# Writing the bf16 copies of the expert weights during the prefix subtiles, and moving a LayerNorm, in a gated-linear-attention and mixture-of-experts layer

## What is computed

```python
# layer 0, x: [4, 4096, 2048] f32
x = x + attn(layernorm(x), Wq, Wk, Wv, Wo, norm_w)
x = x + ffn(layernorm(x), gate_w, w1, w2, w3, ws1, ws2, ws3)

def attn(x, ...):                    # 16 heads of 128 channels, chunks of 64 tokens
    q = silu(x @ Wq.T); f = sigmoid(x @ Wk.T); log_f = log_sigmoid(f); v = x @ Wv.T
    o = chunked_gla(q, v, log_f)     # S_t = diag(exp(log_f_t)) S_{t-1} + outer(1 - exp(log_f_t), v_t)
    return rmsnorm(o, norm_w) @ Wo.T #   o_t = q_t @ S_t, one state S per head

def ffn(x, ...):                     # 8 experts, top 2, and one shared expert, each 2048 -> 1024 -> 2048
    weights, idx = top_k(softmax(x @ gate_w.T), 2)
    y = sum over experts e of comb[:, e] * ((silu(x @ w1[e].T) * (x @ w3[e].T)) @ w2[e].T)
    return y + silu(x @ ws1.T) * (x @ ws3.T) @ ws2.T
```

## Time and profile before

| | us |
|---|---|
| two runs | 8881.81 and 9365.76, median 9123.78 |
| profiled execution | 8866.93 |
| its span, slowest core (core 1) | 8865.2 |
| spans of the eight cores | 8808.3 to 8865.2 |
| busy in the span: TensorE | 5739.3 (65%) |
| VectorE | 2370.4 (27%) |
| ScalarE | 1152.4 (13%) |

### The profile page before, as it was taken

One profiled execution on the slowest core, in us unless ns is written; L12 is line 12 of the kernel. 1 busy time (PEld: TensorE's weight loads), 2 busy tenths in 40 slices (PEclk: granted clock), 3 DMA queues, 4 the chain that ended last, 5 costly groups with the idle time before them and its releaser, 6 DMA issues.

```text
span 8865.2 us, 86241 instructions; the slowest of 8 cores (8808.3 to 8865.2 us)
## 1 busy us (share of the span) xinstructions
PE 5739.3 (65%) x26192; PEld 2628.4 (30%) x26192; DVE 2370.4 (27%) x7284; ACT 1152.4 (13%) x2288; POOL 275.7 (3%) x522
## 2 busy tenths in 40 slices
PE   5454545465565655666677776665877766577877
PEld 3131313232222222232233332322333342233333
DVE  3434343444300100124321112343111124421111
ACT  1111111111100000111111111111111111101111
POOL 0000000000000000000000000000000000000000
PEclk8676767676787878876688998766999986688998
DMA  5131313132577577552243333322333332143332
GB/s 83 32 57 29 60 27 62 30 66 43 104 161 168 136 161 170 132 112 36 41 119 114 114 114 105 67 45 61 124 114 114 114 91 41 31 119 114 114 119 95
DMA packets 203967, 806.76 MB, mean 91 GB/s; under 512 B 22272, under 2 KB 22288, under 8 KB 189200
## 3 DMA queue, kind: packets, MB, share of 16 engines
q0 software_dynamic: 77008, 331.42, 21.9%
q1 hardware_dynamic: 126528, 469.82, 14.6%
HBM read 1002.51 MB, written 130.02 MB: 128 GB/s over the span
## 4 chain that ended last, share of the span: by engine, by line
PE 53%; DVE 16%; DMA 15%; issue 7%; ACT 6%; SPq 2%; DVEq 1%; POOL 1%; ACTq 0%; POOLq 0%
PE ps L76 51%; DMA wB<-w_t 3%; DVE Em L76 3%; DMA wB<-w3c 3%; DMA wC<-w_t 3%; DVE Ssb L76 2%; DVE Ep L76 2%; DVE krem L76 2%; PE psb L76 2%; DMA w2c<-wC 2%; SPq L76 2%; ACT Em L76 2%; ACT krem L76 1%; ACT fm L76 1%; DMA wB<-wk_t 1%
## 5 line engine op out<-in xcount | busy, mean ns | idle before, releaser
L76 PE MATMUL ps<-fm,wA 128*128 128x512 bf16 x5632 | 1497.8, 427 | 917.5 <-DMA wB<-w_t 487.3
L76 PE MATMUL ps<-fm,wB 128*128 128x512 bf16 x6656 | 1758.8, 425 | 37.3 <-DMA wB<-wk_t 26.4
L76 PEld LDWEIGHTS ps<-fm,wA 128*128 128x128 bf16 x5632 | 594.8, 107 | 1764.4 <-issue 1254.8
L76 PEld LDWEIGHTS ps<-fm,wB 128*128 128x128 bf16 x6656 | 702.8, 107 | 1009.1 <-issue 398.4
L76 DVE TENSOR_TENSOR vcb<-sqb,ps 128x512 bf16<-128x512 bf16 x288 | 198.2, 688 | 2671.7 <-PE ps L76 2671.7
L76 PE MATMUL ps<-ob,vcb 128*128 128x512 bf16 x2304 | 623.5, 405 | 262.2 <-ACT Em L76 133.3
L76 DVE SCALAR_TENSOR_TENSOR Ssb<-Ssb,dec,ps 128x128 f32<-128x128 f32 x1024 | 355.7, 347 | 1341.5 <-PE ps L76 1277.6
L76 PE MATMUL ps<-wC,fm 128*128 128x256 bf16 x4096 | 510.9, 291 | 117.3 <-DVE vcb L76 94.4
L76 PE MATMUL ps<-vcb,krtm 64*128 64x128 bf16 x1024 | 247.5, 242 | 502.9 <-ACT krtm L76 246.6
L76 ACT ACTIVATE sqb<-ps 128x512 bf16<-128x512 f32 x352 | 209.6, 595 | 2597.5 <-PE ps L76 2597.5
L76 PE MATMUL ps<-wC,vcb 128*128 128x512 bf16 x2304 | 520.8, 379 | 0.0
(11 more groups left out here) (91 smaller groups left out, 3273.8 us busy)
## 6 DMA issues: line engine op xcount, KB each, us to landing
wA<-w1c SPq DMA_DIRECT2D x216, 512.0 KB, 3.7
wB<-w3c SPq DMA_DIRECT2D x216, 512.0 KB, 4.6
wC<-wv_t POOLq DMA_DIRECT2D x64, 1024.0 KB, 9.4
wB<-wk_t POOLq DMA_DIRECT2D x128, 512.0 KB, 5.3
ob<-w2c SPq DMA_DIRECT2D x108, 512.0 KB, 5.2
wC<-w2c SPq DMA_DIRECT2D x108, 512.0 KB, 8.9
wA<-w_t POOLq DMA_DIRECT2D x72, 512.0 KB, 7.8
wB<-w_t POOLq DMA_DIRECT2D x72, 512.0 KB, 10.7
```

The costliest lines, as they stand in the source:

```text
L76: ins = getattr(eng, name)(*a, **k)
```

## The change

- `_precache_steps` is new. It puts jobs on the queues, 216 in all (matrix, expert, block): POOL loads a block as bf16 into one of four slots of `y1g`, once the store that used the slot four jobs ago and the load just before have landed; SP writes it to the bf16 copy. Seven jobs are queued at the start of every prefix `_pair_chunks`, seven more after the last pair of a prefix subtile.
- All FFN passes load the copies on SP. The loads wait for the write-backs of their blocks. The write-backs of the first pass are gone, and three waits for them.
- `_ffn` computes the LayerNorm of the next own subtile after the gate phase of the last expert, ahead of the w2 phases of experts 7 and 8; it uses the first quarter of `y1g` for the normalised block.
- In the prefix the state slot is chosen by pair and head, not by chunk. `chain_free` is set at the end of every pair. The y1g write of `_rms_wo` waits for the stores.

```diff
+    def _precache_steps(self, nsteps):
+        s = self
+        if s._pc_jobs is None:
+            s._pc_jobs = [(m, e, ic) for e in range(NEXP) for ic in range(8)
+                          for m in range(3)]
+        for _ in range(nsteps):
+            if not s._pc_jobs:
+                return
+            m, e, ic = s._pc_jobs.pop(0)
+            srcs = (s.w1_t, s.w3_t, s.w2_t)[m]
+            dsts = (s.w1c, s.w3c, s.w2c)[m]
+            slot = s._pc_slot
+            s._pc_slot = (slot + 1) % 4
+            stg = s.y1g[:, slot * 2048:(slot + 1) * 2048]
+
+            def ld(gp, srcs=srcs, e=e, ic=ic, stg=stg, slot=slot):
+                gp.wait_ge(s.wbS.h, s._pc_wb[slot])
+                s.pcS.pre(gp)
+                s.pcS.dma(gp.dma_start(stg, srcs[e, ic, :, :]))
+            self.G(ld)
+            tok_ld = s.pcS.n
+
+            def st(sy, dsts=dsts, e=e, ic=ic, stg=stg, tok_ld=tok_ld, slot=slot):
+                sy.wait_ge(s.pcS.h, tok_ld)
+                s.wbS.pre(sy)
+                s.wbS.dma(sy.dma_start(dsts[e, ic, :, :], stg))
+                s._pc_wb[slot] = s.wbS.n
+            self.SY(st)
+            s._pc_done[(m, e, ic)] = s.wbS.n
...
     def _attn_subtile(self, sidx, own):
-        fm_tok, ln_v = self._ln_into_fm0(False, tok_x)
+        if self._fm_pre is not None:
+            fm_tok, ln_v = self._fm_pre
+            self._fm_pre = None
+        else:
+            fm_tok, ln_v = self._ln_into_fm0(False, tok_x)
...
         self._run_pairs(own, fm_tok, vc_tok)
+        if not own:
+            self._precache_steps(7)
...
     def _pair_chunks(self, own, hp, fill, vc_tok):
+        if not own:
+            self._precache_steps(7)
...
     def _pair_post(self, own, hp):
+        s.chain_free = [s.sT.n, s.sT.n]
...
     def _chunk(self, own, h, i, hp, c, ctx, vc_tok):
-        sl = i if own else ((c // 2) % 2) * 2 + i
+        sl = i if own else (hp % 2) * 2 + i
...
         for e in range(NEXP):
             self._gphase(e, fm_tok, tok_comb)
+            if e == NEXP - 1 and self.subcnt in s.xtok:
+                self._fm_pre = self._ln_into_fm0(False, s.xtok[self.subcnt],
+                                                 xt=s.y1g[:, 0:D])
+                self.tag = "expert_w2"
             if e > 0:
                 self._w2phase(e - 1, tok_comb)
...
     def _gphase(self, e, fm_tok, tok_comb):
-            self.G(ld13) if first else self.SY(ld13)
+            stream = s.w13Sh[wbuf]
+            pc_tok = max(s._pc_done.get((0, e, ic), 0), s._pc_done.get((1, e, ic), 0))
+
+            def ld13(sy, e=e, ic=ic, wbuf=wbuf, stream=stream, pc_tok=pc_tok):
+                sy.wait_ge(s.sT.h, max(s.w13_used[wbuf], s.wk_used[wbuf], s.wq_used[wbuf]))
+                sy.wait_ge(s.wbS.h, pc_tok)
+                stream.pre(sy)
+                stream.dma(sy.dma_start(s.wA[:, wbuf * D:(wbuf + 1) * D], s.w1c[e, ic, :, :]))
+                stream.dma(sy.dma_start(s.wB[:, wbuf * D:(wbuf + 1) * D], s.w3c[e, ic, :, :]))
+            self.SY(ld13)
```

More of the change, by code:

```diff
@@ L167, in __init__ @@
         self.wbS = DStream(c, nc, "wbS")
+        self.pcS = DStream(c, nc, "pcS")
+        self._pc_jobs = None
+        self._pc_slot = 0
+        self._fm_pre = None
+        self._pc_done = {}
         self.w2Sh = DStream(c, nc, "w2Sh")
@@ L201, in __init__ @@
         self._wb2_tok = 0
+        self._pc_wb = [0, 0, 0, 0]
         self.y1_tok = 0
@@ L305, in _prefetch_x, with _ln_into_fm0 @@
         self.G(ld)
-    def _ln_into_fm0(self, src_y1, tok_src):
+    def _ln_into_fm0(self, src_y1, tok_src, xt=None):
         self.tag = "ln"
@@ L313, in _ln_into_fm0 @@
         buf = self.subcnt % 2
+        if xt is None:
+            xt = s.vcb[:, s.XTO:s.XTO + D]
         last_v = 0
@@ L365, in norm @@
                 rs = s.lnst[:, 4 * tb + 3:4 * tb + 4]
-                s.sV.inc(v.tensor_scalar(s.vcb[:, s.XTO:s.XTO + D], x_tb, ms, rs, OP.subtract, OP.mult))
+                s.sV.inc(v.tensor_scalar(xt, x_tb, ms, rs, OP.subtract, OP.mult))
             self.V(norm)
@@ L377, in tr @@
                         ins = t.transpose(s.psb[:, kk * 128:(kk + 1) * 128],
-                                          s.vcb[:, s.XTO + k * 128:s.XTO + (k + 1) * 128], s.iden[:, :])
+                                          xt[:, k * 128:(k + 1) * 128], s.iden[:, :])
                     s.sT.inc(ins)
@@ L416, in ld @@
                 gp.wait_ge(s.sT.h, max(s.wv_used[wbuf], s.wo_used[wbuf]))
-                gp.wait_ge(s.wbS.h, s._wb2_tok)
                 s.wvS[wbuf].pre(gp)
@@ L803, in ev @@
             sc.wait_ge(s.iniS.h, 16)
-            sc.wait_ge(s.wbS.h, s._wb2_tok)
             sc.wait_ge(s.sT.h, max(ctx[("omm", i)], s.sq_used, s.w2_used))
@@ L884, in _rms_wo, with ev @@
             tok_mm = s.sT.n
-            def ev(v, g=g, buf=buf, tok_mm=tok_mm, tok_rcol=tok_rcol):
+            def ev(v, g=g, buf=buf, tok_mm=tok_mm, tok_rcol=tok_rcol,
+                   pc_wb=max(s._pc_wb)):
                 v.wait_ge(s.sT.h, tok_mm)
+                v.wait_ge(s.wbS.h, pc_wb)
                 v.wait_ge(s.sV.h, tok_rcol)
@@ L996, in _ldw2, with ldw2 @@
         s = self
[L998 to L1003, removed]
+        stream = s.w2Sh
+        pc_tok = max(s._pc_done.get((2, e, ic), 0) for ic in range(8))
+        def ldw2(sy, e=e, stream=stream, pc_tok=pc_tok):
+            sy.wait_ge(s.sT.h, max(s.w2_used, s.wo_used[0], s.wo_used[1],
                                    s.wv_used[0], s.wv_used[1]))
[L1005 to L1009, removed]
+            sy.wait_ge(s.wbS.h, pc_tok)
+            stream.pre(sy)
             for ic in range(8):
-                src2 = s.w2_t[e, ic, :, :] if first else s.w2c[e, ic, :, :]
-                stream.dma(gp.dma_start(self._w2sl(ic), src2))
-        self.G(ldw2) if first else self.SY(ldw2)
+                stream.dma(sy.dma_start(self._w2sl(ic), s.w2c[e, ic, :, :]))
+        self.SY(ldw2)
         s._w2_ldtok[e] = (stream, stream.n)
[L1015 to L1024, removed]
     def _gphase(self, e, fm_tok, tok_comb):
@@ L1031, in _gphase @@
             wbuf = ic % 2
[L1033 to L1047, removed]
-            self.G(ld13) if first else self.SY(ld13)
-            tok_w = (stream, stream.n)
[L1050 to L1057, removed]
+            stream = s.w13Sh[wbuf]
+            pc_tok = max(s._pc_done.get((0, e, ic), 0), s._pc_done.get((1, e, ic), 0))
+            def ld13(sy, e=e, ic=ic, wbuf=wbuf, stream=stream, pc_tok=pc_tok):
+                sy.wait_ge(s.sT.h, max(s.w13_used[wbuf], s.wk_used[wbuf], s.wq_used[wbuf]))
+                sy.wait_ge(s.wbS.h, pc_tok)
+                stream.pre(sy)
+                stream.dma(sy.dma_start(s.wA[:, wbuf * D:(wbuf + 1) * D], s.w1c[e, ic, :, :]))
+                stream.dma(sy.dma_start(s.wB[:, wbuf * D:(wbuf + 1) * D], s.w3c[e, ic, :, :]))
+            self.SY(ld13)
+            tok_w = (stream, stream.n)
             def hmm(t, ic=ic, wbuf=wbuf, tok_w=tok_w, fm_tok=fm_tok,
```

## The result

| | before | after |
|---|---|---|
| median of all executions | 9282.1 us (10) | 9256.4 us (12) |
| lowest | 8861.9 | 8959.5 |
| profiled execution | 8866.9 | 8959.5 |
| its span, slowest core | 8865.2 | 8958.0 |

The ratio of after to before is 1.0129, 95% interval 1.0073 to 1.0186: slower by more than the measurement's noise, and within 2%. In more than half of all executions of either kernel the cores of one die or both run at a lower granted clock and take some per cent longer; the medians hold them, the ratio and the stage times of these two tables do not.

What follows compares the result with a forecast made beforehand. The first FFN pass was taken as bound by its loads and write-backs. From 8866.9 us, -440.4 there, +503.9 for the prefix's job chain and +18 for the moved LayerNorm gave 8948, say 8950; range 8680 to 9150.

Steps and rivals of the forecast that it cites:

- The sum: Whole kernel: profiled 8866.9 us before, less 440.4, plus 503.9 and 18, gives 8948, say 8950 us, 0.9% slower.
- The first FFN pass falls to the others, -440.4: First FFN pass: reading bf16 copies on SP, it takes the other three passes' mean of 1033.5 us instead of 1473.9.
- The chain, c = 7.1 us, 188c - 831 = +503.9: Prefix: each job load waits for the one before, delaying Wk and Wv; three subtiles grow 145.6 us each, the fourth 67.1.
- c itself: Prefix: cycle of one job, landing plus step to the next issue; 5.8 us without stores, plus 1.2 for a store: 7.1.
- the two Wk loads: Prefix pair loop: two Wk loads add 4.1 us beyond seven job cycles, making 53.8 us a pair against 37.3.
- Rival A: Prefix: a load beside a store lands in 7.8 us, c = 8.4, +748, total 9193 us, slower; chance 0.28.
- B: Prefix: a store costs the load nothing, c = 5.8, +228, total 8673 us, faster; chance 0.13.
- the likeliest case: Whole kernel: c from 5.9 to 7.5, within 2%, 8780 to 9040 us; chance 0.52.
- Rival C: Prefix: jobs run at the engines' busy time, c = 4.6, +34, total 8479 us, much faster; chance 0.07.
- SBUF port contention of POOL's descriptor writing: Prefix: busy VectorE could slow POOL-issued loads; the Skill example would add 2.5 us to c, total about 9420; nothing added.
- State slots 0, chain_free 0: Prefix: slot waits, at most 90 us, hidden while TensorE waits for Wk; chain_free count already passed; both cost 0.
- The moved LayerNorm +6.0 a pass: Three FFN passes: LayerNorm exposed, +37.1, first Wv load no longer hidden, -31.1; +18 us in all, bounds 0 and +42.

Runs made afterwards that it cites:

- the kernel without stores: Changed kernel with its one chain of loads, only expert 0's 24 blocks stored and used by all experts: 8725.4 us.
- the four-stream one: Changed kernel with a separate pair of streams for each y1g slot, so up to four job loads in flight: 8661.6 us in the profiled execution.
- The kernel with the old slots: Kernel with four job loads in flight and SP's single wait, prefix state slots alternating by two chunks as before: prefix subtiles 457.5, 453.8, 455.2 and 440.4 us.

## Why the prediction was right or wrong

Its forecast was 8950 us and "within 2%". The executions behind the ratio took 8959.5, 8970.2, 8980.9, 8983.9 and 9045.4 us; the ratio is 1.0129 where 1.009 was forecast. But the median over all executions, 9256.4, lies outside the range of 8680 to 9150. The step that failed is the choice of the base in "The sum": two runs of before had been shown, 8881.8 and 9365.8, and I put the forecast beside the lower one, on 8866.9, with no term for executions that take longer although the kernel is the same. What the runs showed in its place: the median of before is 9282.1, 415 us above that base, and that of the changed kernel 9256.4, 297 above its own profiled execution. The same sum on the median of before would have given 9364, 107 too much, so the medians of these ten and twelve executions do not show the change at all; the scatter between executions of the changed kernel, 8959.5 to 9599.5, is larger than any term of the sum. The forecast was one of the mechanism, and its terms can be checked one by one. That they add up to within 10 us of the span (8948 and 8958.0) is in part luck: the growth of the prefix is 513 us between the slowest cores and 497 between the means of eight, and of the 19 us in the other stretches 6.9 lie in the last FFN pass (1043.0 for 1036.1), which holds no moved LayerNorm.

- *The first FFN pass falls to the others, -440.4.* Measured -439.1 for the stretch from LayerNorm to LayerNorm, which holds the moved LayerNorm too; the earlier trace rows carried it.
- *The chain, c = 7.1 us, 188c - 831 = +503.9.* Measured +513: 148.6, 152.5, 145.7 and 66.4 where 145.6 three times and 67.1 stood. In the second subtile TensorE waited 30.5 us for Wk of the second pair (24.7 expected), 14.5 to 21.4 us in the third to eighth (16.5), and 19.8 us for Wv (some 20). The first Wk products of the pairs were 54.7 us apart (775.64 to 1103.62 in six pairs), for 53.8.
- *c itself.* Landings of 6.8 us (median of the kernel) and a step of 0.5 give 7.3, so c was 0.2 too small: the store's price is 1.6, and 1.2 had been taken, while the step is 0.1 shorter than the 0.6 that stood in c. In the sum a part of it was given back by the two Wk loads: 54.7 - 7 x 7.3 = 3.6 for the 4.1 us that I put for them. Rival A (7.8 + 0.6) and B (no cost of a store) were both off; the kernel without stores shows what B would have been: +62.5 and +64.7 in the subtiles without any store, for 65. The +228 for B is not 188c - 831, which at 5.8 gives +259: without stores the two Wk loads find 1.3 us more of idle engines in a pair, which the text does not say. Two bounds are off as well: the sum passes 2% at c = 7.61 and not 7.56, and c = 5.9 gives 8723, below the 8780 that is named as the low end of the likeliest case.
- *Rival C*, that the idle DMA capacity is really had, was wrong for this kernel and right for the four-stream one. The idle share was there, and one wait kept it from being used; what C would have had then is 122 us of growth and not 34, since it priced the jobs alone. The landing in a chain without stores was 5.2 us. The rule of the Trainium skill ("DMA: Bandwidth & Descriptors", section "Anatomy of one DMA"), which gave an estimate of 4.4, does not agree with it.
- *SBUF port contention of POOL's descriptor writing*, put at nothing: the kernel without stores has landings of 5.2 us (median, 5.1 at least) in the prefix, with VectorE busy for 175 us of a subtile of 486. Nothing of it is seen. The rule of the Trainium skill ("SBUF — State Buffer", section "Who interferes with whom") has no effect here that the runs can show; which of VectorE's instructions here are in a two-port mode was not looked at.
- *State slots 0, chain_free 0.* The kernel with the old slots shows the first; chain_free was not tried alone.
- *The moved LayerNorm +6.0 a pass.* Measured +9 to +15. The sum was too small here, and the bound of +42 (14 a pass) about right. The mechanism is on the timeline: 36 us of exposed LayerNorm in the new place (3802.6 to 3838.5), 9.8 us for Wv at the end, and up to 12 more in the groups behind it (TensorE waited 21.8 us for Wv in all), for which the bound left some room and the sum none.

## What to carry to other kernels

Idle DMA engines are not idle DMA time: price work that is moved into them by its chain, landing plus the step to the next issue, times its count, against the time between two transfers that the path needs from the same in-order queue. Where that sum is over, a second transfer in flight buys most of it, and after that count the engines' busy time of everything in the stretch, not of the new work alone. Where executions of one kernel scatter by more than the change, name the base of the forecast and give the range room for it. A stage moved on an in-order engine takes its waits with it; only weaving its pieces between other work hides them, and what it used to hide (here a weight load) becomes bare.

## What the runs showed of the hardware

- A 512 KB store beside a converting 1 MB load adds 1.6 us to its landing (6.8 for 5.2), where the store alone keeps the engines busy for 1.3 to 1.4.
- The sixteen DMA engines ran at a share of 0.92 to 0.94 over whole 450 us subtiles with four loads in flight, and Wk loads among them landed in 20 us (median) and not in 5.3; the subtiles were 6 to 9% longer than those of before.
- A wait on SP that is long fulfilled costs about 0.05 us ahead of a DMA issue: 0.36 us between two issues with four waits, 0.21 with one, 0.15 with none.
- With three more such waits ahead of each load, and three more on VectorE in the Wo evacuations, the stretches from one FFN pass to the next were some 18 us longer (1700.4 for 1682.0, mean of eight cores). I had put waits that are long fulfilled at nothing.
